# Experts in slots of 256 rows, norm and gate in one phase, weights in two parts, gathers issued three chunks ahead

## The chip, the cores and the metric

The kernel runs on one core of a Trainium2 chip. The core has TensorE (PE), VectorE (DVE), ScalarE (ACT), GpSimd (POOL) and SyncE (SP), which here only issues DMAs, and 16 DMA engines. The metric is the device time of the whole program in microseconds, 4737.4 us before the change (median of three runs, 4737.3 to 4738.18).

## The reference, cut to what matters

The program is four sub-layers over 4096 tokens of 256 values: linear attention, a feed-forward layer, a selective-scan (Mamba) part of two blocks, and a mixture of eight experts. Each is wrapped as `x = x + _layernorm(f(_layernorm(x)))`. Only the closing norm of the third and the fourth are touched:

```python
x = x + _layernorm(_L1_attn_ref(_layernorm(x), ...))
x = x + _layernorm(_L1_ffn_ref(_layernorm(x), ...))

def _L1_ffn_ref(x, W1, b1, W2, b2, Wg, bg):
    gate_scores = softmax(x @ Wg + bg)                 # 8 experts
    h = relu(einsum('btc,ech->bteh', x, W1) + b1)      # 256 -> 1024
    expert_out = einsum('bteh,ehc->btec', h, W2) + b2  # 1024 -> 256
    topk_scores, topk_idx = top_k(gate_scores, 2)
    top_probs = softmax(topk_scores)
    sel = take_along_axis(expert_out, topk_idx[..., None], axis=2)
    return sum(sel * top_probs[..., None], axis=2)
```

Only the two chosen experts of a token need computing.

## The kernel before

Tokens lie in SBUF as `x_res`, 32 tiles of 128 tokens (`NT`), eight chunks of four tiles (`NCH`, `TPC`). Two spare tiles in front hold zeros. The code is written by hand per engine, with semaphores; each phase (`net.run`) ends in a barrier over all engines, in which SP clears the phase's semaphores, and the next begins with SP setting its counting ones to 1. What stands on an engine runs in the written order.

The Mamba part ends with `stream_out` (`normalise_all` with `back`): the parked input is loaded as one DMA, VectorE takes statistics of all 32 tiles (L116, L120), POOL forms the inverse roots (L1383, L1385), VectorE normalises tile by tile into a double buffer (L1403) and POOL adds the residual chunk by chunk (L1391).

`moe_gate` takes one chunk per turn: statistics and norm again on VectorE (L116 to L1511), transposes on TensorE (L1543), copies on ScalarE (L1533), a small fp32 matmul with the gate weights (L1550), logits on VectorE (L1518). Beside it one expert's weights per chunk (2 MB, two DMAs, L1473 and L1475) are split into a bf16 high part by ScalarE (L1530) and a bf16 rest by VectorE (L1515), which makes nearly fp32 products out of three bf16 matmuls. SP also fills the buffer of rows per expert, `slots_x` in HBM, with zeros (36 DMAs, L1483), between the second and the third expert's weights.

`moe_route` forms top-2, shares and, for each token and choice, a row in `slots_x` (`slot`); each expert's rows start at a multiple of 128, so 72 slots of 128 rows (`NSLOT`) always suffice, and `tile_expert` tells the expert of each. `moe_scatter`: VectorE norms a chunk into `c_xn` (L1691), POOL issues two indirect DMAs per tile (L1711), 64 in all.

`moe_experts` runs one slot per turn, 72 turns. On TensorE: two transposes of the next slot's rows (L1785), the first layer as 48 matmuls of 128 columns, weights stationary (L1815: 8 output blocks, 2 halves of the input, 3 products), in two halves of PSUM banks, then the second layer of the slot before as 24 matmuls of 256 columns, `h` stationary (L1797). The expert's number is read into a register, so the weights' addresses are formed by register instructions. ScalarE adds bias and applies relu (L1848), VectorE makes the bf16 high part and rest of `h` (L1881, L1883). POOL stores each result to `slots_y` (L1771).

`moe_combine`: POOL gathers two rows per token by indirect DMA (L1914, 64 issues), one chunk ahead of VectorE, which weighs and adds them (L1942, L1946), takes statistics, waits for POOL's inverse root (L108, L110), normalises (L1955) and adds to `x_res` (L1960). The inverse root of a chunk stands on POOL behind the gathers of the next. At the end one DMA stores all 4 MB (L1996).

## Time and profile before

| what | us |
|---|---|
| median of the runs | 4737.4 |
| the profiled execution's own time | 4734.2 |
| its span | 4732.5 |
| up to the end of the Mamba blocks (untouched) | 3676 |
| closing norm, then gate phase, up to the routing's first DMA | 161.9 |
| routing, up to the first scatter issue | 27.4 |
| scatter, up to TensorE's first instruction of the expert loop | 95.9 |
| expert loop on TensorE | 631.2 |
| from there to the first gather issue | 13.5 |
| gathers and sums, up to the store's issue | 112.5 |
| the store, to the end of the span | 14.0 |
| combine, VectorE per chunk: weighted sums and statistics (4706.11 to 4710.69) | 4.6 |
| combine, VectorE per chunk: norm and addition (4712.34 to 4714.98) | 2.6 |
| combine, POOL: eight gathers and one root, the pitch of a chunk (4628.91 to 4641.54) | 12.6 |
| ScalarE, cast of 128x256 out of PSUM, mean | 0.37 |

The times of stages are differences of start times in the timeline of the one profiled execution. A row's duration is the instruction's own; what an engine waited for stands behind it in brackets. Matmuls overlap, so their pace is read from the difference of their starts, not from their durations.

### The profile page before, as it was taken

How to read it: one execution, taken by the hardware profiler on the slowest of the kernel's cores; microseconds unless marked ns; L12 is line 12 of the kernel's file. 1: busy time of each engine (PE TensorE's matmuls, PEld its weight loads, DVE VectorE, ACT ScalarE, POOL GpSimd, SP SyncE). 2: the span in 40 equal slices, each digit the busy share in tenths (PEclk: the TensorE clock that was granted, in tenths of full speed). 3: DMA queues.
4: the chain of work that ended last, by engine and by line, in shares of the span. 5: the costliest groups of instructions: out<-in, count | busy, mean ns of one | idle time of the engine just before them, and what ended most of it. 6: DMA issues, size and time to landing. Idle time of an engine off the chain costs nothing. (4 is left out here: it accounts for less than half of the span.)

```text
span 4732.5 us, 95080 instructions
## 1 busy us (share of the span) xinstructions
PE 3637.2 (77%) x29740; PEld 2399.9 (51%) x29741; DVE 2779.8 (59%) x4894; ACT 2001.0 (42%) x4694; POOL 2035.8 (43%) x1225
## 2 busy tenths in 40 slices
PE   6888869838988888888569888888888124888870
PEld 3545546525555555555345555555555123666650
DVE  3444423347777777777557777777776542333324
ACT  2121212136666665656256656565664111323220
POOL 1010100026666666667356767676767223000016
PEclk9878769969999999999779999999999557999995
DMA  1000000111213121312121312121221521000003
GB/s 47 0 0 0 0 20 0 35 44 48 73 48 74 48 74 48 74 48 71 33 64 48 74 48 71 49 72 50 65 57 51 204 87 66 29 29 31 29 30 100
DMA packets 156158, 241.76 MB, mean 51 GB/s; under 512 B 26450, under 2 KB 84082, under 8 KB 153076
## 3 DMA queue, kind: packets, MB, share of 16 engines
q1 hardware_dynamic: 146164, 210.61, 16.4%
q0 software_dynamic: 9600, 26.23, 1.6%
q8 instruction: 207, 3.39, 0.3%
q14 instruction: 187, 1.53, 0.1%
HBM read 118.86 MB, written 36.18 MB: 33 GB/s over the span
## 5 line engine op out<-in xcount | busy, mean ns | idle before, releaser
L893 POOL TENSOR_TENSOR m_hc<-m_h,m_Cb 128x1024 f32<-128x1024 f32 x512 | 1204.9, 2354 | 764.5 <-DVE m_h L1014 446.7
L1014 DVE TENSOR_TENSOR_SCAN m_h<-m_dA,m_hlast,m_bank 128x256 f32<-128x256 f32 x2048 | 1355.0, 727 | 142.8 <-PE m_bank L1295 61.5
L1277 PE MATMUL m_bank<-m_hc,ident 128*128 128x512 f32 x2048 | 1206.0, 678 | 146.3 <-POOL m_hc L893 146.0
L1144 ACT ACTIVATE m_dA<-m_delta,m_rate 128x256 f32<-128x256 f32 x2048 | 894.1, 500 | 15.6 <-DVE m_h L1014 14.7
L1293 PEld LDWEIGHTS m_bank<-m_M,m_U 128*128 128x128 bf16 x8192 | 607.6, 101 | 359.9 <-DVE m_h L1014 220.6
L1293 PE MATMUL m_bank<-m_M,m_U 128*128 128x64 bf16 x8192 | 677.9, 197 | 123.5 <-DVE m_h L1014 112.2
L1295 PEld LDWEIGHTS m_bank<-m_M,m_U 112*128 112x128 bf16 x8192 | 581.2, 101 | 204.8 <-issue 172.8
L1295 PE MATMUL m_bank<-m_M,m_U 112*128 112x64 bf16 x8192 | 678.3, 197 | 0.0
L1277 PEld LDWEIGHTS m_bank<-m_hc,ident 128*128 128x128 f32 x2048 | 338.7, 205 | 195.4 <-POOL m_hc L893 162.8
L1771 POOL DMA_DIRECT2D slots_y<-x_y x72 | 39.0, 541 | 609.8 <-DVE x_y L1870 609.8
L962 DVE SCALAR_TENSOR_TENSOR m_cv<-m_xpre,m_conv,m_cv 128x256 f32<-128x256 f32 x384 | 273.5, 754 | 22.5 <-ACT m_cv L1082 18.0
L1207 PE MATMUL m_bank<-m_pair,m_in 128*128 128x256 f32 x1024 | 268.8, 389 | 8.1 <-ACT m_cv L1082 4.4
L1815 PE MATMUL x_bank<-x_xhi,r_wlo 128*128 128x128 bf16 x1152 | 262.3, 228 | 13.4 <-DVE x_xlo L1861 0.4
L1848 ACT ACTIVATE x_h<-x_bank,x_b 128x128 f32<-128x128 f32 x576 | 164.7, 368 | 225.4 <-PE x_bank L1815 225.3
L1207 PEld LDWEIGHTS m_bank<-m_pair,m_in 128*128 128x128 f32 x1024 | 194.7, 194 | 120.2 <-issue 94.1
L1815 PE MATMUL x_bank<-x_xhi,r_whi 128*128 128x128 bf16 x1152 | 250.6, 218 | 0.0
L1815 PE MATMUL x_bank<-x_xlo,r_whi 128*128 128x128 bf16 x1152 | 249.6, 217 | 0.1
L108 POOL TENSOR_SCALAR var_eps<-a_mv 128x4 f32<-128x4 f32 x16 | 3.7, 229 | 520.3 <-DVE a_mv L120 520.3
L1881 DVE CAST x_hhi<-x_h 128x512 bf16<-128x512 f32 x144 | 61.5, 427 | 273.2 <-ACT x_h L1848 273.2
L1797 PE MATMUL x_bank<-r_whi,x_hlo 128*128 x576 | 157.6, 274 | 58.6 <-DVE x_hlo L1883 58.4
L398 PE MATMUL a_bank<-a_qh,a_phi 128*128 128x512 f32 x256 | 142.8, 691 | 48.3 <-DVE a_qh L233 38.8
L844 POOL TENSOR_TENSOR m_Mlo<-m_Mf,m_Mhi 128x1024 bf16<-128x1024 f32 x64 | 166.3, 2598 | 6.6 <-ACT m_Mhi L1125 6.6
(262 smaller groups left out, 5747.6 us busy)
## 6 DMA issues: line engine op xcount, KB each, us to landing
m_Cb<-m_c_rows SPq DMA_DIRECT2D x256, 256.0 KB, 3.2
m_M<-m_Mhi SPq DMA_DIRECT2D x128, 256.0 KB, 4.1
m_M<-m_Mlo SPq DMA_DIRECT2D x64, 256.0 KB, 3.9
m_U<-m_Uhi SPq DMA_DIRECT2D x128, 128.0 KB, 3.2
g_stage<-in_e_w SPq DMA_DIRECT2D x16, 1024.0 KB, 6.9
slots_x<-x_res SPq DMA_DIRECT2D x36, 256.0 KB, 4.2
x_x_in<-slots_x SPq DMA_DIRECT2D x72, 128.0 KB, 2.0
slots_y<-x_y POOLq DMA_DIRECT2D x72, 128.0 KB, 2.0
```

The source lines that it names most:

```text
L844: nc.gpsimd.tensor_tensor(Mlo[:, j], Mf[:, j], Mhi[:, j], ALU.subtract).then_inc(s["mlo_done"], 1)
L893: nc.gpsimd.tensor_tensor(hc[:, n % 2], h[:, n % RING], Cb[:, g % 2, n % NG, :].unsqueeze(1).broadcast_to([P, KI, CM]), ALU.mult).then_inc ...
L962: i = nc.vector.scalar_tensor_tensor(cv[:, m, :], xpre[:, m, k:k + CM], conv[:, m, k:k + 1], cv[:, m, :], ALU.mult, ALU.add)
L1014: nc.vector.tensor_tensor_scan(h[:, n % RING, m, :], dA[:, n % RING, m, :], VB[(n % 2) * 2 + g][:, (m % 2) * CM:(m % 2 + 1) * CM], hlast[: ...
L1144: nc.scalar.activation(dA[:, n % RING, m, :], delta[:, par, m, :], ACT.Exp, scale=rate[:, m, n:n + 1]).then_inc(s["da_done"], 1)
L1207: last = nc.tensor.matmul((H0, H1)[g % 2][:, m % 2 * CM:(m % 2 + 1) * CM], w_in[:, k, m * P:(m + 1) * P], xT[:, k, :], start=(k == 0), sto ...
L1277: last = nc.tensor.matmul(Y[half][:], net.ident[:], hc[:, n % 2, 2 * half:2 * half + 2, :], start=(n == 0), stop=(n == NS - 1))
L1293: nc.tensor.matmul(bank[:, at:at + SUB], U1[:, par, j, m * P:(m + 1) * P], M1[:, par, j, n, :], start=True, stop=False)
L1295: last = nc.tensor.matmul(bank[:, at:at + SUB], U2[:, par, j, m * P:(m + 1) * P], M2[:, par, j, n, :], start=False, stop=True)
L1797: last = nc.tensor.matmul(YB[par][:, 0:D], h_part[:, par, m * P:(m + 1) * P], w_part[:, bass.ts(e * (WB // 2) + KD * KH // 2 + m, D)], sta ...
L1815: last = nc.tensor.matmul(HB[par][b][:, at:at + P], w_part[:, bass.ts(e * WB + kk * KH + m, P)], x_part[:, par, kk * P:(kk + 1) * P], star ...
L1848: last = nc.scalar.activation(h[:, par, m * P:(m + 1) * P], HB[par][b][:, at:at + P], ACT.Relu, bias=b1[:, bass.ts(e * KH + m, 1)])
```

## The change

- **Slots of 256 rows** (`SLOT`), 40 of them; two slots per round, 20 rounds. TensorE runs both first layers (each 48 matmuls of 256 columns in four groups of two output blocks, each group a PSUM bank), each followed by the four transposes of its slot of the next round, then both second layers (each 48 matmuls of 256 columns). Eight banks as before, but `h` is kept in fp32 only for two groups.
- **Norm, residual and gate in one phase**, chunk by chunk, written out without loops: first statistics, root, normalisation on ScalarE in place, residual added by POOL, second statistics, root, rows for the gate. `stream_out` goes. With each chunk goes one 1 MB piece of weights, eight pieces, the first four experts. The zero fills (now 40) are issued behind the last piece.
- **The other eight pieces** are loaded and split in the scatter phase, the subtraction on VectorE (`low`) between the norms of tiles. The scatter goes tile by tile with 12 buffers.
- **Combine**: gathers run three chunks ahead, straight from `slot`, into a buffer for all tiles; VectorE sums chunk c before it finishes chunk c − 1; each finished chunk is stored at once, in place of the one store at the end.

The diff, cut to what matters:

```diff
-    net.run(lambda n: stream_out(n, parked))
...
-NSLOT = 2 * NT + NE
+
+SLOT = 2 * P
+NSLOT = NT + NE
 WB = (KD * HID + KH * D) // P
 IDX = mybir.dt.int32
+EARLY = NE
+
+
+def expert_weights(net, ctx, tag, whi, wlo, pieces):
+
+    dram = net.dram
+    W1 = KD * HID
+    stage = net.sb(ctx, tag + "stage", [P, 2, W1])
+    loaded = [net.own(f"{tag}weights{par}") for par in range(2)]
+    hi_done, lo_done = net.sem(tag + "hi_done"), net.sem(tag + "lo_done")
+    cols = lambda i: slice(pieces[i] * W1, (pieces[i] + 1) * W1)
+
+    def load(sp, i):
+        if i >= 2:
+            sp.wait_ge(lo_done, 1 + i - 1)
+        of = dram[("e_w1", "e_w2")[pieces[i] % 2]][pieces[i] // 2]
+        sp.dma_start(stage[:, i % 2, :], of.rearrange("p a b -> p (a b)")).then_inc(loaded[i % 2], 16)
+
+    def high(act, i):
+        act.wait_ge(loaded[i % 2], (i // 2 + 1) * 16)
+        net.nc.scalar.copy(whi[:, cols(i)], stage[:, i % 2, :]).then_inc(hi_done, 1)
+
+    def low(dve, i):
+        dve.wait_ge(hi_done, 1 + i + 1)
+        net.nc.vector.tensor_tensor(wlo[:, cols(i)], stage[:, i % 2, :], whi[:, cols(i)], ALU.subtract).then_inc(lo_done, 1)
+
+    return load, high, low
...
+                for c in range(NCH):
+                    if c >= 2:
+                        sp.wait_ge(s["sum_done"], 1 + c - 1)
+                    sp.dma_start(residual[:, c % 2], chunk(net.parked, c)).then_inc(s[f"back{c % 2}"], 16)
+                    load(sp, c)
+                sp.wait_ge(s["zero_set"], 1 + 1)
+                filled = slots_x.rearrange("(i p r) d -> i p r d", p=P, r=SPARE)
+                for i in range(NSLOT * SLOT // (P * SPARE)):
+                    sp.dma_start(filled[i], net.x_all[:, 0:SPARE, :]).then_inc(s["zeroed"], 16)
+                sp.wait_ge(s["zeroed"], NSLOT * SLOT // (P * SPARE) * 16)
...
+                def root(c):
+                    pool.wait_ge(s["stats"], 1 + c + 1)
+                    if c == 1:
+                        pool.wait_ge(s["root"], 1 + 1)
+                    elif c >= 2:
+                        pool.wait_ge(s["root2"], 1 + c - 1)
+                    inverse_root(net, pool, rstd[:, c % 2], mv[:, c % 2, :, 1]).then_inc(s["root"], 1)
+
+                def add(c):
+                    pool.wait_ge(s["normal"], 1 + c + 1)
+                    pool.wait_ge(s[f"back{c % 2}"], 16 * (c // 2 + 1))
+                    nc.gpsimd.tensor_tensor(chunk(x, c), chunk(x, c), residual[:, c % 2], ALU.add).then_inc(s["sum_done"], 1)
+
+                def root2(c):
+                    pool.wait_ge(s["stats2"], 1 + c + 1)
+                    pool.wait_ge(s["root"], 1 + min(c + 2, NCH))
+                    pool.wait_ge(s["root2"], 1 + c)
+                    inverse_root(net, pool, chunk2(rstd2, c), chunk(mv2, c)[:, :, 1]).then_inc(s["root2"], 1)
+
+                root(0)
+                root(1)
+                for c in range(NCH):
+                    add(c)
+                    root2(c)
+                    if c + 2 < NCH:
+                        root(c + 2)
...
+                first(0)
+                first(1)
+                shifts(0)
+                for c in range(NCH):
+                    if c + 1 < NCH:
+                        shifts(c + 1)
+                    second(c)
+                    if c + 2 < NCH:
+                        first(c + 2)
+                    low(dve, c)
+                    rows(c)
+                    if c >= 1:
+                        logits(c - 1)
+                logits(NCH - 1)
...
+                normal(0)
+                for c in range(NCH):
+                    if c + 1 < NCH:
+                        normal(c + 1)
+                    high(act, c)
+                    if c >= 1:
+                        turned(c - 1)
+                turned(NCH - 1)
...
-                after(V.tensor_scalar(tiles[:], tiles[:], float(P), -1.0, ALU.mult, ALU.add))
+                after(V.tensor_scalar(tiles[:], tiles[:], float(SLOT), -1.0, ALU.mult, ALU.add))
...
+            def _(pool):
+                for t in range(NT):
+                    pool.wait_ge(ready, 1 + t + 1)
+                    for i in range(2):
+                        nc.gpsimd.indirect_dma_start(slots_x, bass.IndirectOffsetOnAxis(slot[:, t, i:i + 1], 0),
+                                                     xn[:, t % HELD, :], None).then_inc(sent[t % HELD], 16)
...
+                for t in range(NT):
+                    if t >= HELD:
+                        dve.wait_ge(sent[t % HELD], t // HELD * 32)
+                    nc.vector.tensor_scalar(xn[:, t % HELD, :], x[:, t, :], mv[:, t, 0:1], rstd[:, t:t + 1],
+                                            ALU.subtract, ALU.mult).then_inc(ready, 1)
+                    if t >= HELD and t % 2 == 0 and (t - HELD) // 2 < PIECES:
+                        low(dve, (t - HELD) // 2)
+                for i in range((NT - HELD) // 2, PIECES):
+                    low(dve, i)
...
+    PAIRS, T2 = NSLOT // 2, SLOT // P
+    GROUPS = KH // 2
...
+                def layer1(i, par, e, first):
+                    pe.wait_ge(s[f"xlo_done{par}"], 1 + i + 1)
+                    for g in range(GROUPS):
+                        if par == 1:
+                            pe.wait_ge(s["h_done0"], 1 + i * GROUPS + g + 1)
+                        elif not first:
+                            pe.wait_ge(s["h_done1"], 1 + (i - 1) * GROUPS + g + 1)
+                        pe.sem_inc(net.carrier, 1)
+                        for m in (2 * g, 2 * g + 1):
+                            out = HB[g][:, m % 2 * SLOT:(m % 2 + 1) * SLOT]
+                            for kk in range(KD):
+                                for n, (w_part, x_part) in enumerate(PARTS_X):
+                                    last = nc.tensor.matmul(out, w_part[:, bass.ts(e * WB + kk * KH + m, P)],
+                                                            x_part[:, par, kk, :],
+                                                            start=(kk == 0 and n == 0), stop=(kk == KD - 1 and n == 2))
+                        last.then_inc(s[f"h_psum{par}"], 1)
+
...
+                def body(i, first, last_round):
+                    e = [expert(pe, i * 2 + par) for par in range(2)]
+                    for par in range(2):
+                        layer1(i, par, e[par], first)
+                        if not last_round:
+                            turn(i + 1, par, False)
+                    for par in range(2):
+                        layer2(i, par, e[par], first)
+
...
+    LEAD_Q = 3
...
+                for c in range(NCH):
+                    sp.wait_ge(x_done, 1 + c + 1)
+                    tiles = slice(c * TPC, (c + 1) * TPC)
+                    sp.dma_start(out_rows[:, tiles, :], x[:, tiles, :]).then_inc(stored, 16)
+                sp.wait_ge(stored, NCH * 16)
...
+                for c in range(LEAD_Q):
+                    gather(c)
+                for c in range(NCH):
+                    if c + LEAD_Q < NCH:
+                        gather(c + LEAD_Q)
+                    root(c)
...
+                sums(0)
+                for c in range(1, NCH):
+                    sums(c)
+                    result(c - 1)
+                result(NCH - 1)
...
-                sp.dma_start(out.rearrange("(n p) d -> p n d", p=P), net.x).then_inc(stored, 16)
```

How the instructions stand on each engine. On TensorE, at the start of the expert loop, before (`x_xhi`, `x_xlo` are the two parts of the rows, `r_whi`, `r_wlo` those of the weights; ISA and REGISTER_ALU form the address of the weights):

```order
L1785 MATMUL x_bank<-ident,x_x_in 128x128 x2
L1748 TENSOR_LOAD r_tile_expert
L1748 ISA x2
L1785 MATMUL x_bank<-ident,x_x_in 128x128 x2
L1815 ISA
L1815 MATMUL x_bank<-x_xhi,r_wlo 128x128
L1815 REGISTER_ALU
L1815 MATMUL x_bank<-x_xlo,r_whi 128x128
L1815 MATMUL x_bank<-x_xhi,r_whi 128x128
```

and the same place now:

```order
L1879 MATMUL x_bank<-ident,x_x_in 128x128 x8
L1835 TENSOR_LOAD r_tile_expert
L1835 ISA x2
L1835 TENSOR_LOAD r_tile_expert
L1835 ISA x2
L1895 ISA
L1895 MATMUL x_bank<-x_xhi,r_wlo 128x256
L1895 REGISTER_ALU
L1895 MATMUL x_bank<-x_xlo,r_whi 128x256
L1895 MATMUL x_bank<-x_xhi,r_whi 128x256
```

The triple of matmuls is the same with twice the columns; both experts' numbers are read ahead of it.

On VectorE, in the gate phase, one chunk before (`g_st`, `g_mv` are statistics):

```order
L120 BN_AGGR g_mv<-g_st 128x2 x4
L1506 REGISTER_ALU
L1507 ISA
L1507 COPY r_mv<-g_mv 128x8
L1509 ISA
L1509 COPY r_rstd<-g_rstd 128x4
L1511 TENSOR_SCALAR g_xn<-x_res,g_mv,g_rstd 128x256 x4
L1515 ISA
L1515 TENSOR_TENSOR r_wlo<-g_stage,r_whi 128x4096
L1518 ISA
L1518 TENSOR_TENSOR r_gate<-g_bank,g_bg 128x32
```

and one chunk now:

```order
L1555 SCALAR_TENSOR_TENSOR g_shift<-g_mv,g_rstd 128x4
L1562 BN_STATS g_st<-x_res 128x6 x4
L1566 BN_AGGR r_mv<-g_st 128x2 x4
L1546 BN_STATS g_st<-x_res 128x6 x4
L1550 BN_AGGR g_mv<-g_st 128x2 x4
L1442 TENSOR_TENSOR r_wlo<-g_stage,r_whi 128x2048
L1574 TENSOR_SCALAR g_xn<-x_res,r_mv,r_rstd 128x256 x4
L1579 TENSOR_TENSOR r_gate<-g_bank,g_bg 128x32
```

Two statistics blocks stand in a chunk, the first of them (L1562) behind POOL's addition of the residual, and the weights' subtraction is half as long and stands ahead of the rows.

On POOL, in the combine phase, before:

```order
L1914 DMA q_got<-slots_y,q_at 128x256 x8
L1923 UNCONDITIONAL_BRANCH
L1923 ISA
L1914 DMA q_got<-slots_y,q_at 128x256 x8
L1919 REGISTER_ALU
L107 ISA
L108 TENSOR_SCALAR var_eps<-q_mv 128x4
L110 TENSOR_TENSOR q_rstd<-var_eps,minus_half 128x4
```

and now:

```order
L2027 DMA q_got<-slots_y,r_slot 128x256 x32
L107 ISA
L108 TENSOR_SCALAR var_eps<-q_mv 128x4
L110 TENSOR_TENSOR q_rstd<-var_eps,minus_half 128x4
L2027 DMA q_got<-slots_y,r_slot 128x256 x8
```

The first root stands behind 32 gathers instead of 16, and so the root of the fifth chunk behind the last gather.

## Rows read from the trace of the kernel before

**Rows 1.** The page, granted TensorE clock in 40 equal slices, tenths of full speed.
```profile
PEclk9878769969999999999779999999999557999995
```

**Rows 2.** Timeline of VectorE, POOL and SP: start, duration (us), engine, line, operation, releaser.
```profile
3676.16 10.55 DVE L116 BATCH_NORM_STATS2 so_st<-x_res 128x6 f32<-128x256 f32 x32 [5.24 <-PEq L85]
...
3699.95 2.42 DVE L1403 TENSOR_SCALAR so_tmp<-x_res,so_mv,so_rstd 128x256 f32<-128x256 f32 x1
3699.78 2.44 POOL L1391 TENSOR_TENSOR x_res<-so_residual,so_tmp 128x1024 f32<-128x1024 f32 x1 [0.87 <-DVE so_tmp L1403]
...
3727.09 33.68 SPq L1483 DMA_DIRECT2D slots_x<-x_res  x36
3728.35 1.41 DVE L116 BATCH_NORM_STATS2 g_st<-x_res 128x6 f32 x4 [8.76 <-DMA g_bg<-in_e_bg]
3730.77 1.04 POOL L110 TENSOR_TENSOR g_rstd<-var_eps,minus_half 128x4 f32<-128x4 f32 x1
...
3747.58 4.42 DVE L1515 TENSOR_TENSOR r_wlo<-g_stage,r_whi 128x4096 f32 x1
3753.77 0.19 DVE L1518 TENSOR_TENSOR r_gate<-g_bank,g_bg 128x32 f32 x1 [1.76 <-PE g_bank L1550]
...
3838.02 0.34 SPq L1580 DMA_DIRECT2D o_rank<-in_rank  x1
```

**Rows 3.** Busy time of a 5 us window in the fills; last two columns DMA share, GB/s.
```profile
3745.00:3750.00 5.00, 1.96 (x8) 1.57 (x8) 3.79 (x6) 1.07 (x2) 1.04 (x1) 0.50 1.05 403
```

**Rows 4.** Expert loop: its window (PE, PEld, DVE, ACT, POOL, PEclk), two groups, TensorE's timeline.
```profile
3961.30:4592.50 631.20, 541.50 (x5321) 429.15 (x5322) 221.93 (x431) 191.44 (x648) 38.43 (x71) 1.00 0.09 29
...
L1883 DVE TENSOR_TENSOR x_hlo<-x_h,x_hhi 128x512 bf16<-128x512 f32 x144 | 99.7, 693 | 5.0
L1881 DVE CAST x_hhi<-x_h 128x512 bf16<-128x512 f32 x144 | 61.5, 427 | 273.2 <-ACT x_h L1848 273.2
...
4107.67 0.27 PE L1797 MATMUL x_bank<-r_whi,x_hhi 128*128 x1
4108.02 0.41 PE L1785 MATMUL x_bank<-ident,x_x_in 128*128 128x128 f32 x2
4108.53 0.23 PE L1815 MATMUL x_bank<-x_xhi,r_wlo 128*128 128x128 bf16 x1
...
4110.46 0.22 PE L1815 MATMUL x_bank<-x_xhi,r_whi 128*128 128x128 bf16 x1
4110.78 0.23 PE L1815 MATMUL x_bank<-x_xhi,r_wlo 128*128 128x128 bf16 x1
...
4111.02 0.23 PE L1815 MATMUL x_bank<-x_xhi,r_wlo 128*128 128x128 bf16 x1
...
4113.95 0.27 PE L1797 MATMUL x_bank<-r_whi,x_hhi 128*128 x1
...
4114.28 0.27 PE L1797 MATMUL x_bank<-r_whi,x_hhi 128*128 x1
```

**Rows 5.** POOL's timeline in the scatter, its first and its last issue.
```profile
3865.39 1.47 POOL L1711 DMA_INDIRECT slots_x<-c_xn,c_at  x1 [26.70 <-DVE c_xn L1691]
...
3945.79 0.96 POOL L1711 DMA_INDIRECT slots_x<-c_xn,c_at  x1 [0.30 <-issue]
```

**Rows 6.** Combine: timeline of VectorE, POOL and SP.
```profile
4605.96 1.02 POOL L1914 DMA_INDIRECT q_got<-slots_y,q_at  x1 [10.48 <-DVE q_at L1934]
...
4628.85 1.23 DVE L1960 TENSOR_TENSOR x_res<-x_res,q_z 128x1024 f32 x1 [0.16 <-DVE q_z L1955]
4628.91 2.00 POOL L1914 DMA_INDIRECT q_got<-slots_y,q_at  x1 [0.30 <-issue]
...
4700.73 0.95 POOL L1914 DMA_INDIRECT q_got<-slots_y,q_at  x1 [0.30 <-issue]
...
4718.49 0.40 SPq L1996 DMA_DIRECT2D out_x<-x_res  x1
```

537 lines of the change are left out of this document (250 added, 287 removed).

## The prediction

> **What bounds the kernel now.** The profile was read from its coarse views to its fine ones. In the row of the granted clock the reader is to see the last nine of the 40 slices: two at 0.5, one at 0.7, five at 0.9 or more, one at 0.5 [rows 1]. They are the expert part, the only one that the diff touches; attention, feed-forward and Mamba take the 3676 us before. Inside these last 1056 us the timeline gives the stages. The closing norm of the Mamba part starts at 3676.2, the gate phase runs to about 3836, the routing begins at 3838.0 [rows 2], the scatter's DMA issues run from 3865.4 to 3946.8 [rows 5], the expert loop on TensorE from 3961.3 to 4592.5 [rows 4], the gathers from 4606.0 to 4701.7, and one store of 4 MB, issued at 4718.5, fills the rest [rows 6]. Each stage ends in a barrier, so gains add up, and each has its own limit:
>
> - Norm and gate: VectorE, POOL and DMA in turns. A single VectorE TENSOR_SCALAR that normally takes 0.33 us took 2.42 us while POOL added a chunk for 2.44 us [rows 2]: the two exclude each other. 36 fills of 256 KB occupy the queue for 33.7 us, at about 403 GB/s [rows 2, 3], with later weight loads behind them.
> - Scatter and gathers: POOL's issue, 0.96 us busy and 0.30 us idle in the one, 0.95 and 0.30 in the other, so 1.26 and 1.25 us each [rows 5, 6].
> - Experts: TensorE. One turn is 128 rows. A first-layer triple of 128-column matmuls takes 0.25 us (4110.78 to 4111.02), though three bare steps are 0.16 at 128 columns; a second-layer triple of 256 columns takes 0.33 us (4113.95 to 4114.28) [rows 4]. So twice the columns cost only a third more. In the loop the clock is at 1.00, the higher level (2.4 GHz).
>
> **The change, part by part** (all against the profiled run, span 4732.5, own time 4734.2; the median of the runs is 4737.4, 3.2 more, and I take the same difference for the new kernel).
>
> **1. Experts.** Before: 72 turns of 128 rows in 631.2 us, 8.77 each. Now 40 slots of 256 rows, two per round, 20 rounds: 10240 rows instead of 9216, so 11% more padding is paid. Per slot: 16 first-layer triples and 16 second-layer triples, all of 256 columns. The first-layer form with 256 columns is not in the trace. Its bounds are 0.25 us per triple (the 128-column row, which it can't beat) and 0.33 plus the 0.09 by which the 128-column triple exceeds its three bare steps, 0.42. I take 0.327, the second-layer row: the instruction pattern with one register step per triple is the same, and there it costs nothing beside 256 columns. 16 × 0.327 = 5.23 us for either layer. Waits: from the end of one group of matmuls to the next the row shows 0.32 us instead of 0.08 to 0.11 (4110.46 to 4110.78) [rows 4], so +0.22 per wait; three inner ones per slot make 0.66. Transposes: two take 0.51 us until the next matmul (4108.02 to 4108.53), plus 0.24 ahead of them (0.35 from the matmul at 4107.67, less its own 0.11) [rows 4]; four I take as 1.0. One round: 2 × (5.23 + 0.66) + 0.22 + 2 × 1.0 + 2 × (0.22 + 5.23) + 0.6 for branch and register loads = 25.5 us, times 20 = 510 us. **−121 us.** The wait ahead of each second layer for the half of hlo just made goes, since both first layers now stand ahead of both second layers (it needs no term: the round is counted anew). What is late next must be VectorE: cast 0.43 and subtraction 0.69 per group [rows 4], 1.15 us against 1.5 us of TensorE, and 5.2 us of second layer lie ahead of the one that needs the last group. So it stays covered. If it were not, 1 us per round returns, 20 us. Ends: 459 us (no wait costs anything: 4 × 5.23 + 1.7 + 0.35 per round) and 510 + 32 × 20 × 0.09 = 568 us (0.42 per first-layer triple).
>
> **2. Norm, residual and gate in one.** The closing norm with its barrier (3676.2 to 3723.6) disappears as a phase, its work goes into the gate's chunks. First 4.7 us until the small loads land (as 3723.6 to 3728.35), two statistics blocks of 1.83 (1.41 plus the aggregation), root, four normalisations on ScalarE (about 1.5, from 0.37 for a cast of this shape, see the table), one addition 2.44 [rows 2]: the second statistics of chunk 0 start 12.8 us in. Then a cycle through POOL and VectorE: add 2.44, second statistics 1.83, first statistics of the chunk after next 1.83, weights' subtraction 2.25 (half of the 4.42 row), root 1.36, four hops of 0.2: 10.5 us. The subtraction is in it because its two SBUF inputs hold POOL off; the evidence is weaker than for TENSOR_SCALAR, it is the gather that took 2.00 instead of 0.95 us beside a TENSOR_TENSOR [rows 6]. Without it the cycle is 8.3. The SP queue issues the eighth piece after the sixth subtraction, at 12.8 + 5 × 10.5 + 5.9 = 71.2, and only behind it the fills, now 40 instead of 36: 10.5 MB at 403 GB/s are 26.0 us, with the piece before (2.6) and 2.5 until the last lands: 102.3. The last chunk's logits: second statistics at 84.3 (the seventh round is 2 short), 6.8 to the rows' end, 6.4 through transposes and gate matmuls (as 3747.6 to 3753.96): 98. So fills end it, just, and the routing starts at 3676.1 + 102.3 + 2.3 = 3780.7 instead of 3838.0: **−57 us**, ends −47 (cycle 12.5) and −68 (cycle 8.3).
> The Trainium skill, page "SBUF — State Buffer", in the table on the bandwidth-pool intuition, gives HBM to core about 358 GB/s; by it the fills would take 29.3 instead of 26.0 us and the stage would gain 54. The row shows 403, so the sum goes by the row.
>
> **3. Routing.** Two operations shrink from 576 to 320 elements: −0.7 us.
>
> **4. Scatter.** Still 64 issues at 1.27 = 81 us, starting 1 us earlier as one tile is enough to begin. New beside them: 8 MB of weights (20 us of DMA at 403 GB/s, on another queue, landing early), and on VectorE eight subtractions of 2.25 us with two SBUF inputs. The gather at 4628.91 began 0.06 us after such an operation of 1.23 us and took 1.05 us longer [rows 6]; a subtraction that begins while an issue is in flight would hold the next for about 1.7 us. 8 × 1.7 = 14. **+13 us**; ends 0 and +18 (8 × 2.25). What waits behind: the next scatter issues; VectorE has 12 tiles of lead.
> Here a page speaks for another result: the Trainium skill, "SBUF — State Buffer", section "Who interferes with whom", says that a tensor_tensor takes only the read interface of the pair shared with GpSimd while descriptor generation needs the write interface (marked as inferred), so such a DMA would not be stalled. By it this term is −1 and the time 14 less; the 2.00 us row speaks against it.
>
> **5. Combine and store.** POOL issues three chunks ahead. No index copies: first issue at about 4605.2 in old time. 64 × 1.25 = 80, and four roots instead of six ahead of the last gather, each with what it drags along 2.65 us (12.65 us per eight gathers and a root, see the table): ends at 4695.8 instead of 4701.7. But root(4) now stands behind the last gather, and VectorE has more left: root 1.5, results of four chunks at 2.7, sums of two at 4.6 (both from the table), hops: 22.1, ending at 4717.9. Before, the sums ended 3 us earlier, then came a barrier and the store's issue at 4718.5, with 14.0 us to the end of the span. Now only the last 512 KB follow the last sum: 0.2 + 3.5 (1.3 at 403 GB/s, the rest latency, an estimate) + 1.6 for the barrier: 4723.2 against 4732.5. **−9 us**, ends −4 and −14.
>
> **6. Barriers.** About 50 more semaphores are set and cleared on SP, at some 0.05 us each (estimate from stage changes of 1.6 us with about 17 of them and 2.3 with 22); part of it is in the terms: +2 us.
>
> Sum: −121 − 57 − 1 + 13 − 9 + 2 = −173. Span 4559.5, own time about 4561, median 4737.4 − 173 = **4564 us**.
>
> **Rivals.**
> - *TensorE's waits vanish behind longer matmuls.* 256 columns give the sequencer slack of 0.08 us per triple, and it may run ahead past a met wait. Against it: before each turn, after 24 such matmuls, there is still a gap of 0.24 (with a register load in it). Experts 459: 4564 − 51 = 4513.
> - *The register step stays visible with 256 columns,* as weights rather than moving operand depend on it. Against: the step is short of the slack. 568: 4564 + 58 = 4622.
> - *A TENSOR_TENSOR does not hold POOL off:* scatter 14 less, gate cycle 8.3 instead of 10.5, which brings the fills 11 forward: 4539. The 2.00 us row [rows 6] speaks against it, gathers beside two-input SCALAR_TENSOR_TENSOR that lose nothing speak for it. The Trainium skill's rule for the scatter is the one named in part 4.
> - *Slower than before: TensorE falls to the lower of its two clocks (1.2 GHz, granted 0.5) in the expert loop.* Matmuls are 418 us of the 510; at half clock 836, total 928: 4982. The point is a mean granted clock of 0.71, where 418/0.71 + 92 reaches the 683 us that eat the whole gain. In the old loop it is at 1.00 [rows 4] although TensorE idles 1 us in each turn; the new one idles less. Hence small.
> - *The change does not do what it says:* a weight piece or a gather that is not covered holds its stage. The largest would be the eight late pieces outside the scatter, 8 × (2.6 + 1.8 + 2.25) = 53 us: 4617. They need 35 us of an 81 us stage.
>
> **How the numbers follow.** Forecast 0.66 (4535 to 4600), waits vanish 0.12, the register step 0.07, POOL not held off 0.09, uncovered pieces 0.03, clock 0.02, other 0.01. The range takes the first four cases nearly whole: 4510 to 4620. Something near 0.2% is what a measurement can tell here. Faster 0.97, same 0.01, slower 0.02.
>
> **What would show it.** Right: second-layer and first-layer triples both near 0.33, a round near 25.5 us, 20 rounds near 510; fills that start about 71 us into the gate stage and end it; scatter issues of up to 3 us beside subtractions; a VectorE tail of about 22 us after the last gather; a last store of 512 KB. Wrong: a triple at 0.25 or above 0.4, gate cycles of 8, scatter issues all at 0.96, a granted clock below 1 in the loop.

## The result, and the profile after

The changed kernel takes **4497.4 us** (median of 4 runs, 4491.8 to 4501.8) against 4737.8 us (4 runs, 4737.3 to 4746.5) for the kernel before on the same chip: ratio 0.9487, 95% interval 0.9473 to 0.9501, 240 us less. Forecast were 4564 us and a range of 4510 to 4620. The direction was right, the size was not: 67 us more were gained, 13 us beyond the range's end. The profiled execution took 4501.8 us, with a span of 4500.1 us and a mean granted clock of 0.866.

The granted clock of the changed kernel, in 40 slices of 112.5 us, to be held against [rows 1]; the last seven and a third of the one before are its expert part:

```profile
PEclk8888878968999999999978999999999985599995
```

The time in front of the expert part varies from one execution to the next, although no kernel here touches it: in the profiles of this case Mamba's last addition ends between 3667.1 and 3689.3 us. So stages are compared from that point on. Each figure is read from the traces of before and after; the first row counts from the end of that addition, the last one to the end of the span, all else from start to start.

| Stretch | before | after | difference | forecast |
|---|---|---|---|---|
| end of Mamba's last addition to the routing's first DMA | 167.1 | 108.1 | −59.0 | −57 and part of +2 |
| to the first scatter issue | 27.4 | 25.1 | −2.3 | −2 |
| to TensorE's first work of the expert loop | 95.9 | 108.8 | +12.9 | +14 |
| expert loop on TensorE, to its last matmul | 631.9 | 449.7 | −182.2 | −121 |
| to the first gather | 12.8 | 11.4 | −1.4 | 0 |
| first gather to the end of the span | 126.5 | 117.2 | −9.3 | −9 |
| sum | 1061.6 | 820.3 | −241.3 | −173 |

Five of six lines hit to within 3 us. **The expert loop alone missed, by 61 us.** The window view of both loops (length, then busy us and instructions of PE, PEld, DVE, ACT and POOL, granted clock, DMA share, GB/s), before and then after; the last line is one whole round of after, from the start of one round's first matmul to that of the next:

```profile
3961.30:4593.40 632.10, 542.40 (x5328) 429.78 (x5328) 221.93 (x431) 191.44 (x648) 38.43 (x71) 1.00 0.09 29
```

```profile
3921.80:4371.70 449.90, 443.90 (x4000) 393.36 (x4000) 227.88 (x399) 153.30 (x360) 21.13 (x39) 0.99 0.14 45
4105.80:4128.09 22.29, 22.00 (x200) 19.55 (x201) 11.40 (x21) 7.66 (x18) 1.08 (x2) 1.00 0.14 47
```

Before, TensorE was busy for 542 of 632 us, after for 444 of 450, and for 22.00 of 22.29 in a round. The clock is the higher level (2.4 GHz) in both, but for the first stretch of each loop: in after the first 28 matmuls of the first layer start 0.213 us apart at a granted 0.50, later ones 0.109 at 1.00. The timeline of after's TensorE shows where the idle time is gone (start, duration, line, operation; the rows to look at are the starts of a first layer, its transposes and what follows them; where rows are left out, triples repeat every 0.33 us):

```profile
4105.80 0.28 PE L1895 MATMUL x_bank<-x_xhi,r_wlo 128*128 128x256 bf16 x1 [0.30 <-issue]
4106.14 0.27 PE L1895 MATMUL x_bank<-x_xhi,r_wlo 128*128 128x256 bf16 x1
...
4110.72 0.27 PE L1895 MATMUL x_bank<-x_xhi,r_wlo 128*128 128x256 bf16 x1
4110.94 0.27 PE L1895 MATMUL x_bank<-x_xhi,r_whi 128*128 128x256 bf16 x1
4111.05 0.60 PE L1879 MATMUL x_bank<-ident,x_x_in 128*128 128x128 f32 x4
4111.48 0.27 PE L1895 MATMUL x_bank<-x_xhi,r_wlo 128*128 128x256 bf16 x1
...
4116.72 0.60 PE L1879 MATMUL x_bank<-ident,x_x_in 128*128 128x128 f32 x4
4117.16 0.27 PE L1908 MATMUL x_bank<-r_whi,x_hlo 128*128 x1
```

The 16 triples of a first layer take 5.25 us (4105.80 to 4111.05) and no wait between them shows; the four transposes take 0.43 us until the next matmul; the only gap of a round stands at its start, where two experts' numbers are loaded: 0.30 us of idle engine, and 0.43 us more from one matmul's start to the next than elsewhere. Round: 5.25 + 5.24 + 10.48 for the matmuls, 2 × 0.44 + 0.43, together 22.3 us, the pitch at which rounds start in the trace.

The gate stage of after, one cycle of VectorE and POOL (in square brackets the idle time ahead of an instruction and what ended it), to be held against [rows 2]:

```profile
3716.61 1.39 DVE L1562 BATCH_NORM_STATS2 g_st<-x_res 128x6 f32<-128x256 f32 x4
...
3720.61 2.29 DVE L1442 TENSOR_TENSOR r_wlo<-g_stage,r_whi 128x2048 bf16<-128x2048 f32 x1 [0.50 <-ACT r_whi L1438]
3720.72 3.20 POOL L110 TENSOR_TENSOR g_rstd<-var_eps,minus_half 128x4 f32<-128x4 f32 x1
...
3722.82 3.45 DVE L1574 TENSOR_SCALAR g_xn<-x_res,r_mv,r_rstd 128x256 f32<-128x256 f32 x4
3722.93 0.33 SPq L1434 DMA_DIRECT2D g_stage<-in_e_w  x1
3723.78 2.34 POOL L1520 TENSOR_TENSOR x_res<-x_res,g_residual 128x1024 f32<-128x1024 f32 x1
...
3726.36 1.39 DVE L1562 BATCH_NORM_STATS2 g_st<-x_res 128x6 f32<-128x256 f32 x4
```

One cycle is 9.75 us (3716.61 to 3726.36). POOL's TENSOR_TENSOR of the root, 1.04 us when alone, takes 3.20 beside the subtraction; four TENSOR_SCALARs, 1.38 us when alone, take 3.45 beside POOL's addition.

### The profile page after: what moved, and what is told of

Same layout as the page of the kernel before. It is cut to its first block and busy times, and to the rows that moved or that the text cites. A ratio compares the mean times of both kernels' runs of the same rounds, so it can differ in the third digit from the quotient of the medians.

```text
span 4500.1 us, 88368 instructions
## 1 busy us (share of the span) xinstructions
PE 3545.9 (79%) x28412; PEld 2364.2 (53%) x28413; DVE 2771.5 (62%) x4814; ACT 1979.1 (44%) x4446; POOL 2045.3 (45%) x1206
## 5 line engine op out<-in xcount | busy, mean ns | idle before, releaser
L1949 ACT ACTIVATE x_h<-x_bank,x_b 128x256 f32<-128x256 f32 x320 | 134.1, 470 | 285.8 <-PE x_bank L1895 278.2
L1863 POOL DMA_DIRECT2D slots_y<-x_y x40 | 21.7, 542 | 446.2 <-DVE x_y L1990 446.2
L1895 PE MATMUL x_bank<-x_xhi,r_wlo 128*128 128x256 bf16 x640 | 176.1, 275 | 6.0 <-issue 5.0
L1895 PE MATMUL x_bank<-x_xlo,r_whi 128*128 128x256 bf16 x640 | 175.8, 275 | 0.0
L1895 PE MATMUL x_bank<-x_xhi,r_whi 128*128 128x256 bf16 x640 | 175.8, 275 | 0.0
L1908 PE MATMUL x_bank<-r_whi,x_hhi 128*128 x640 | 174.4, 273 | 0.0
L1908 PE MATMUL x_bank<-r_wlo,x_hhi 128*128 x640 | 174.4, 273 | 0.0
L1908 PE MATMUL x_bank<-r_whi,x_hlo 128*128 x640 | 174.4, 273 | 0.0
```

Source lines behind the costliest of these rows:

```text
L1895: last = nc.tensor.matmul(out, w_part[:, bass.ts(e * WB + kk * KH + m, P)], x_part[:, par, kk, :], start=(kk == 0 and n == 0), stop=(kk == ...
L1908: last = nc.tensor.matmul(YB[par][:, t * D:(t + 1) * D], h_part[:, par, m, t * P:(t + 1) * P], w_part[:, bass.ts(e * (WB // 2) + KD * KH / ...
L1949: last = nc.scalar.activation(h[:, g % 2, m % 2, :], HB[g][:, m % 2 * SLOT:(m % 2 + 1) * SLOT], ACT.Relu, bias=b1[:, bass.ts(e[par] * KH + ...
```

## The experiments

Twelve kernels were run. First the expert loop, since it holds the miss.

**Theory** formed from the trace of after: TensorE has two limits, its stream of instructions and the columns that its matmuls pass. In the old first layer the stream was the slower one (0.25 us for each triple with its register steps), so that every wait and register load came on top. With 256 columns the matmuls are the slower one (0.327), the stream runs ahead, and what it has beside matmuls vanishes. **Rivals:** the gain comes from the order of the round (two first layers ahead of two second ones), or waits became cheap for another reason.

**Half the columns, shared addresses.**

```diff
+ for half in range(2):
+     rows = slice(half * P, (half + 1) * P)
      for kk in range(KD):
          for n, (w_part, x_part) in enumerate(PARTS_X):
-             last = nc.tensor.matmul(out, w_part[:, bass.ts(e * WB + kk * KH + m, P)], x_part[:, par, kk, :], ...)
+             last = nc.tensor.matmul(out[:, rows], w_part[:, bass.ts(e * WB + kk * KH + m, P)], x_part[:, par, kk, rows], ...)
```

> The new kernel with every first-layer matmul of 256 columns split into two of 128 (96 instead of 48 per slot, same products, same weights loaded twice). Theory A (the old first layer was paced by its instructions, 0.25 us per triple whatever the columns below 256): 32 triples of 0.25 per slot instead of 16 of 0.327, 8.0 instead of 5.2 us, plus waits between groups that show again at 0.2 us each; over 40 slots the expert loop grows from 450 to about 560 to 590 us. Theory B (the gain of the loop comes from the new order of the layers, not from the wider matmuls): the columns are the same, the loop stays within 10 us of 450.

Measured: 4510.9 us, ratio 0.9517 (0.9475 to 0.9559); expert loop 456.7 instead of 449.7 us. A triple of 128 columns now starts every 0.17 us (TensorE's timeline):

```profile
4109.01 0.22 PE L1897 MATMUL x_bank<-x_xhi,r_wlo 128*128 128x128 bf16 x1
...
4109.18 0.22 PE L1897 MATMUL x_bank<-x_xhi,r_wlo 128*128 128x128 bf16 x1
...
4109.34 0.22 PE L1897 MATMUL x_bank<-x_xhi,r_wlo 128*128 128x128 bf16 x1
```

This looked as if my theory had fallen: the same 128 columns, and no 0.25. But the order of TensorE's instructions shows what the edit did beside it. The second half reuses the addresses of the first, so a pair of register steps (one ahead of the first matmul of a triple, one behind it) stands only in the first two of the four triples of an output block. A round's first rows fit: there the triples with the pair start 0.25 and 0.22 us apart, the first matmul of each 0.11 ahead of the second, where 0.06 is usual, and the even 0.17 comes behind them:

```profile
4108.37 0.23 PE L1897 MATMUL x_bank<-x_xhi,r_wlo 128*128 128x128 bf16 x1 [0.29 <-issue]
4108.48 0.22 PE L1897 MATMUL x_bank<-x_xlo,r_whi 128*128 128x128 bf16 x1
...
4108.62 0.23 PE L1897 MATMUL x_bank<-x_xhi,r_wlo 128*128 128x128 bf16 x1
...
4108.84 0.22 PE L1897 MATMUL x_bank<-x_xhi,r_wlo 128*128 128x128 bf16 x1
```

The run changed two things at once and told nothing on the pair. So a second run gave each half a register of its own.

**Half the columns, an address pair for each triple.**

```diff
  def layer1(i, par, e, first):
+     e1 = (e, expert(pe, i * 2 + par))
      ...
-     w_part[:, bass.ts(e * WB + kk * KH + m, P)]
+     w_part[:, bass.ts(e1[half] * WB + kk * KH + m, P)]
```

> The changed kernel with its first layer in halves of 128 columns, as in the earlier run with halves, but the second half computes its weight addresses from a register of its own: one pair of register steps for each triple of matmuls, as in the kernel before; the earlier run shared a pair between two triples. One more register load per slot comes with it. Theory A (TensorE's own instruction stream paces the old first layer; a register pair takes about 0.17 us of it, three matmuls alone little): every triple of 128 columns at 0.25 us, a slot's first layer at 8.0 instead of 5.3, the expert loop 40 x 2.7 = 110 us above the changed kernel's 450 us, so 550 to 570. Theory B (something else in the old loop, its PSUM banks or its waits, made the triple 0.25): triples stay at 0.165, the loop within 20 us of 457.

Measured: 4671.9 us, ratio 0.9854 (0.9827 to 0.9881); expert loop **618.9 us**, 162 more than with shared addresses and nearly the 631.9 of the old kernel. Timeline of its TensorE, one first layer:

```profile
4109.69 0.23 PE L1898 MATMUL x_bank<-x_xhi,r_wlo 128*128 128x128 bf16 x1
...
4109.94 0.23 PE L1898 MATMUL x_bank<-x_xhi,r_wlo 128*128 128x128 bf16 x1
...
4110.18 0.23 PE L1898 MATMUL x_bank<-x_xhi,r_wlo 128*128 128x128 bf16 x1
...
4110.70 0.23 PE L1898 MATMUL x_bank<-x_xhi,r_wlo 128*128 128x128 bf16 x1
...
4117.39 0.63 PE L1879 MATMUL x_bank<-ident,x_x_in 128*128 128x128 f32 x4
...
4118.44 0.23 PE L1898 MATMUL x_bank<-x_xhi,r_wlo 128*128 128x128 bf16 x1 [0.42 <-issue]
```

Triples are back at 0.25 us. And with them everything else is back: from one group to the next 0.52 instead of 0.25 us, so 0.27 for the wait; from the transposes to the next matmul 1.05 instead of 0.43 us. Per slot 32 × 0.087 = 2.8, three waits 0.8, transposes with the register loads 0.6, together 4.2 against 162.2 / 40 = 4.05 us measured. Theory A's 550 to 570 us was thus too low. The waits' surplus was expected in neither theory's number (110 us), but it follows from the first: a stream that paces the loop exposes all it holds. The sizes I had put into the forecast, 0.22 for a wait and 1.0 for the transposes, are those of such a loop.

The two runs bound the stream's costs, by this reading. Four triples with four pairs take 1.0 us, with two pairs no more than 0.66, so a pair costs at least 0.17 us and three matmuls at most 0.08 of the stream.

**More waits, in the changed kernel and in the one before.** TensorE waits again, for something long done, and increments a semaphore behind it, as at a group's start: four more times per slot in the one (160 in all), six more per turn in the other (432). A wait below is always the two together.

```diff
  # after, ahead of each m
+ if m % 2:
+     pe.wait_ge(s[f"xlo_done{par}"], 1 + i + 1)
+     pe.sem_inc(net.carrier, 1)
  # before, ahead of each m
+ if m % (KH // 2):
+     pe.wait_ge(s["xlo_done"], 1 + k + 1)
+     pe.sem_inc(net.carrier, 1)
```

> The new kernel with one more wait that is already met, and one more semaphore increment, in the middle of each first-layer group on TensorE: 4 more per slot, 160 in all. If a met wait costs 0.22 us wherever it stands (the prediction's step), the loop grows by 35 us to 485. If the sequencer runs ahead behind matmuls of 256 columns, it stays within 3 us of 450.

> The old kernel with the same addition ahead of each output block of the first layer but the first of a half: 6 per turn, 432 in all, behind matmuls of 128 columns. If the price of a met wait shows only where TensorE is paced by its instructions, the loop grows by about 0.2 x 432 = 90 us, from 631 to 720. If a met wait costs nothing in either kernel and the 0.22 us gap has another cause (the change of bank), it stays at 631.

Measured: after 4511.3 us, loop 457.9 (+8.2, **0.05 us** per wait); before 4807.7 us, ratio 1.0143 (1.0083 to 1.0203), loop 700.2 (+68.3, **0.16 us** per wait). The first lies between the two forecasts of 453 and 485, the second near the 720 of its first one. A step from one output block (m) to the next in the old kernel, and the places at which the new one lets a gap show (0.18 to 0.19 where a step is 0.11, at most once in four triples, at a group's start):

```profile
4100.37 0.23 PE L1818 MATMUL x_bank<-x_xhi,r_wlo 128*128 128x128 bf16 x1
...
4100.77 0.23 PE L1818 MATMUL x_bank<-x_xhi,r_wlo 128*128 128x128 bf16 x1
```

```profile
4107.86 0.27 PE L1898 MATMUL x_bank<-x_xhi,r_whi 128*128 128x256 bf16 x1
4108.05 0.28 PE L1898 MATMUL x_bank<-x_xhi,r_wlo 128*128 128x256 bf16 x1
```

In the old kernel each wait shows. In the new one, by the same reading of the two limits, four triples have 4 × (0.327 − 0.25) = 0.31 us of slack: one wait fits, two of 0.16 to 0.22 just don't, and 0.07 us of them shows. A met wait is thus not free behind 256 columns; it has a budget, and the changed kernel stays within it.

**The order of the round.** Each slot's second layer stands right behind its first layer and the next transposes, instead of both first layers ahead of both second ones.

```diff
  for par in range(2):
      layer1(i, par, e[par], first)
      if not last_round:
          turn(i + 1, par, False)
- for par in range(2):
      layer2(i, par, e[par], first)
```

> The new kernel with the second layer of a slot directly behind its first layer and the transposes. The last group's relu (0.84), cast and subtraction (1.2) and two hops then stand between first and second layer, less the transposes' 0.45: about 2 us per slot, 80 us over 40 slots. Theory A (pace of instructions is the main source of the gain): the loop grows to about 530 us, and the old kernel's own wait for the subtraction, 58 us, is the part of the gain that order explains. Theory B (order is the main source): the loop loses most of its 181 us gain, 600 us or more.

Measured: 4625.3 us, ratio 0.9758 (0.9717 to 0.98); loop 566.9, +117.2 us or 2.93 per slot. The waits of its TensorE (total us, times, longest), of a stretch with 37 slots:

```profile
PE x_bank L1908 <- DVE x_hlo L1980: 88.7, 37, 2.8
PE x_bank L1895 <- issue: 4.9, 17, 0.3
```

The loop lies between the two theories' 530 and 600 us. 105 of the 117 us stand between the transposes and the second layer, 2.63 per slot, most of it the way of the last group through ScalarE and VectorE (the view counts 2.40 as idle, as it lets the transposes' ends run on). Another 13 us lie inside the second layers: behind some of the pauses the granted clock was 0.50, the lower level, and about 130 matmuls start 0.21 instead of 0.11 us apart (4302.3 to 4305.4, 4316.1 to 4319.2 and others). So the order is needed: without it a good part of the gain is gone. The rival is thus true in part. The kernel before had its second layer a turn late and still waited for the halves of h, as the same view of its loop shows (here of a stretch with 66 such waits):

```profile
PE x_bank L1797 <- DVE x_hlo L1883: 54.7, 66, 0.9
```

That is 0.83 us per turn, and it is gone in the changed kernel, which has no wait for x_hlo in its loop.

**The loop's account.** With an address pair for each triple, and all else of the changed kernel, 128 rows take 618.9 / 80 = 7.74 us against 8.78 before: order, groups and the lost wait give 72 × 1.04 = 75 us. The 8 more half slots (40 × 2 against 72 turns) take back 8 × 7.74 = 62. Sharing the address gives 162, and 256 columns in one matmul instead of twice 128 give 7. Together −182 us, as measured. By this account the step from 128 to 256 columns is worth 169 us, and nearly all of it is the half as many register pairs and what they had exposed. The trace agrees: between the run with shared addresses and the one with an address for each triple, 135 of the 162 us lie inside the first layers, and most of the rest where they begin, behind the transposes and at the start of a round.

**VectorE's subtraction beside POOL.** Two edits leave the subtraction out of one stage; the low halves of those eight weight pieces are zero then, set by ScalarE. First beside the scatter:

```diff
- if t >= HELD and t % 2 == 0 and (t - HELD) // 2 < PIECES:
-     low(dve, (t - HELD) // 2)
  ...
  for i in range(PIECES):
      high(act, i)
+     blank(act, i)
```

> The new kernel without the eight subtractions of VectorE in the scatter phase: ScalarE writes zeros to the low parts of the last four experts' weights instead, so that the result is less exact. If the subtractions hold POOL's issues off (eight issues of 2.1 to 2.8 instead of 0.96 us), the 64 issues take 81 us again and the time falls by 12 to 13 us. If they cost through DMA traffic of the weights, which is unchanged here, it stays.

Measured: 4493.3 us, ratio 0.9474 (0.9444 to 0.9504); from the first scatter issue to the last 80.0 instead of 92.1 us, 12.1 less or 1.51 per subtraction. The issues of the scatter in after, beside the subtraction at 3821.47, and then the row of all scatter issues without it (shortest, median and longest in ns):

```profile
3820.88 0.96 POOL L1778 DMA_INDIRECT slots_x<-c_xn,r_slot  x1 [0.30 <-issue]
3822.14 2.44 POOL L1778 DMA_INDIRECT slots_x<-c_xn,r_slot  x1 [0.30 <-issue]
3824.89 2.54 POOL L1778 DMA_INDIRECT slots_x<-c_xn,r_slot  x1 [0.31 <-issue]
3827.73 0.96 POOL L1778 DMA_INDIRECT slots_x<-c_xn,r_slot  x1 [0.30 <-issue]
```

```profile
L1781 POOL DMA_INDIRECT slots_x<-c_xn,r_slot x64: 956/961/1248, 3819.9 to 3899.9; - x64
```

The page "SBUF — State Buffer" of the Trainium skill, section "Who interferes with whom", has such a DMA unstalled beside a tensor_tensor (it marks the reason as inferred). Here it is stalled; the measurement decides.

The same in the gate stage, twice: first with ScalarE zeroing the halves in the gate stage itself, then with the zeroing moved to the scatter stage.

```diff
  # the first attempt
- low(dve, c)         # VectorE
+ blank(act, c)       # ScalarE, behind high(act, c)
  # the second
- low(dve, c)
+ skip(dve, c)        # the wait and the semaphore of low, without the subtraction
```

> The same in the gate phase for the first eight pieces (low parts written as zeros by ScalarE). If POOL's root and addition wait for the subtraction, the cycle of a chunk falls from 9.75 to about 8 us, the fills start 9 to 11 us earlier and the time falls by about 10. If the cycle is set by something else it stays near 9.75.

> The changed kernel with the weights' subtraction left out of the gate stage on VectorE (only its wait and its semaphore stay); the low halves of these eight pieces are set to zero by ScalarE in the scatter stage, where it has room, so that no engine of the gate stage gets work in exchange. The result lacks these low parts. Theory A (the subtraction takes 2.3 us of VectorE and holds POOL's root for 2.2 us, so that the addition falls on the normalised rows): the gate cycle falls from 9.75 us to about 7.5, the fills start 12 to 16 us earlier and the stage ends with the last logits, about 15 us earlier. Theory B (the cycle runs through ScalarE and TensorE anyway): the cycle falls by less than 1 us, the stage by less than 7.

The first attempt measured 4496.6 us, ratio 0.9496 (0.9474 to 0.9519), and a cycle of 10.6 us, longer than with the subtraction. It was a poor experiment: ScalarE's zeroing (1.91 us a piece) lies in a chain from ScalarE's copy of the turned rows through TensorE and VectorE's logits back to ScalarE. Its timeline, and then that of the second attempt, one cycle each:

```profile
3702.79 1.40 DVE L1565 BATCH_NORM_STATS2 g_st<-x_res 128x6 f32<-128x256 f32 x4
...
3706.68 1.91 ACT L1445 ACTIVATE r_wlo<-g_stage 128x2048 bf16<-128x2048 f32 x1
...
3713.21 0.19 DVE L1582 TENSOR_TENSOR r_gate<-g_bank,g_bg 128x32 f32<-128x32 f32 x1 [5.55 <-PE g_bank L1640]
3713.39 1.40 DVE L1565 BATCH_NORM_STATS2 g_st<-x_res 128x6 f32<-128x256 f32 x4
```

```profile
3725.21 1.40 DVE L1566 BATCH_NORM_STATS2 g_st<-x_res 128x6 f32<-128x256 f32 x4
3733.83 0.19 DVE L1583 TENSOR_TENSOR r_gate<-g_bank,g_bg 128x32 f32<-128x32 f32 x1 [0.99 <-PE g_bank L1641]
3734.01 1.40 DVE L1566 BATCH_NORM_STATS2 g_st<-x_res 128x6 f32<-128x256 f32 x4
```

The second attempt: 4497.1 us, ratio 0.9486 (0.9461 to 0.9511); the cycle is 8.80 us instead of 9.75, the fills start 8.1 us earlier and the scatter 7.8 us earlier. So a subtraction is worth 1 us in the gate stage, not its 2.3, because the chain through TensorE is only 1 us shorter than VectorE's: the logits' instruction (3725.03) and a shift of 0.15, then on ScalarE 2.08 (norm), 1.88 (high part of the weights) and 1.06 (turned rows), then 3.58 of gate matmuls, for which the next logits wait. The cycle falls by less than 1 us, as theory B had it; the stage by a little more than its 7.

**What can still be gained.** Fills between the weight loads, and each chunk's root ahead of the next gathers, first alone, then both; last with four instead of eight weight pieces in the gate stage.

```diff
  # gate stage, sync queue
+ if c >= 1:
+     for i in range((c - 1) * FILLS // (NCH - 1), c * FILLS // (NCH - 1)):
+         sp.dma_start(filled[i], net.x_all[:, 0:SPARE, :]).then_inc(s["zeroed"], 16)
  # combine, gpsimd
+ root(c)
  if c + LEAD_Q < NCH:
      gather(c + LEAD_Q)
- root(c)
  # the last of the four runs
- EARLY = NE
+ EARLY = NE // 2
- if t >= HELD and t % 2 == 0 and (t - HELD) // 2 < PIECES:
-     low(dve, (t - HELD) // 2)
+ if HELD <= t < HELD + PIECES:
+     low(dve, t - HELD)
```

> The new kernel with the 40 zero fills issued behind the weight pieces 1 to 7, five or six each, instead of behind the last. DMA is busy for a third of a cycle there. If the fills bound the gate phase, it ends with the last logits, about 8 us earlier. If the fills delay the residual and the weights by 3.5 us per chunk and the chain has no slack for it, the cycle grows and the gain is lost.

> The new kernel with the inverse root of chunk c ahead of the gathers of chunk c + 3 instead of behind them. The tail of VectorE behind the last gather is 21 us now; with one root more ahead of the last gather (2.7 us) it should shrink to about 14: 4 to 5 us less in all. If the tail is set by the gathers' landing, nothing changes.

> The changed kernel with both edits that gained alone: the fills issued between the gate stage's weight loads, and the root of each chunk ahead of the next gathers. From the end of the Mamba part to the end of the span they gave 811.4 and 815.5 us against 820.3. If they add up, 806.5 here, and 14 us less than the changed kernel in the median; if the earlier routing makes the one edit worth nothing, 811.

> Fills between the weight loads and roots first, as in the run below, and only four weight pieces instead of eight in the gate stage; the other twelve beside the scatter, one subtraction behind each of the tiles 12 to 23. If a subtraction costs 1.5 us of POOL's time beside the scatter, four more cost 6 us there; four gate cycles without one gain 4 x 2 = 8 us if the cycle falls to 7.7. So 0 to 5 us faster than the run below; slower by 5 to 10 if the twelve pieces do not arrive in time behind the tiles.

| Kernel | median us | ratio, 95% | Mamba's end to the scatter | scatter issues | last gather to the end | Mamba's end to the end |
|---|---|---|---|---|---|---|
| changed kernel | 4497.4 | 0.9487 (0.9473–0.9501) | 133.2 | 92.1 | 26.8 | 820.3 |
| fills between | 4487.1 | 0.9474 (0.9452–0.9496) | 125.1 | 92.2 | 26.8 | 811.3 |
| root first | 4489.8 | 0.9488 (0.946–0.9515) | 133.2 | 91.6 | 19.4 | 815.4 |
| both | 4488.0 | 0.9458 (0.9435–0.9481) | 125.1 | 92.6 | 19.4 | 807.2 |
| both, four early | 4488.1 | 0.9463 (0.9441–0.9485) | 119.1 | 98.4 | 19.4 | 806.9 |

The rows come from three chips; each ratio is against the kernel before on the same chip, so the medians are not to be compared by the microsecond. Inside the traces the two edits give 9.0 and 4.8 us and together 13.1, so they add up; in the traces the four forecasts (8, 4 to 5, together 806.5 left, and 0 to 5) all hold to within 1 us. The root first shortens the tail by 7.3 us and lengthens the gathers from 90.4 to 93.2. Four pieces moved gain 6.1 us ahead of the scatter and lose 5.8 in it (4 × 1.51 = 6.0): nothing. The issues of the fills in the changed kernel, and with them between the loads (first and last start):

```profile
L1502 SPq DMA_DIRECT2D slots_x<-x_res x40: 355/646/1548, 3752.6 to 3781.6; - x40
```

```profile
L1505 SPq DMA_DIRECT2D slots_x<-x_res x40: 344/542/967, 3681.3 to 3748.5; - x40
```

The last logits of that run are done at 3769.86 us, 21 us after the last fill's issue, and now end the stage. In the medians these gains of 5 to 13 us are near the spread of single runs (4476 to 4498 for both together), which comes mostly from the part ahead of Mamba's end. The version with both edits is the one to keep, by its trace; by its runs alone its interval overlaps that of the changed kernel.

## Why the prediction was right and wrong

- **What bounds the kernel: mostly right.** Of TensorE it said that twice the columns cost a third more, which held. It read the 0.25 us of a triple off [rows 4] without asking which of two limits that was, and this is the root of the miss.
- **Experts, −121 forecast, −182 measured: wrong.** The step that failed is the working of the round, "+0.22 per wait" and all that was counted like it. Its triples were right: 0.327 us in both layers. Nine waits (1.98 us, of which nothing shows), the transposes (2 × 1.0 where 0.44 was measured, 1.1 too many) and the branch with its register loads (0.6 against 0.43) were sizes of a loop paced by instructions, carried into one paced by columns. They make 3.2 us per round, 25.5 against 22.3, and 64 us in 20 rounds. 3.7 us came back, from ends that I had not counted: 2.9 us pass before the first round's first layer, and that round takes 24.9 us, since its first 28 matmuls run at the lower clock level; the last two rounds, the very last without transposes, are 1.9 us short together.
- **The argument against the right rival failed too.** "Before each turn, after 24 such matmuls, there is still a gap of 0.24" was taken as proof that a wait shows behind 256 columns. But there [rows 4] a register load stood with it, and the stream can have had little lead, since the turn's first layer was paced by it (this is a reading; no run takes that gap apart). In the changed kernel a gap with register loads is left too, 0.43 us, once per round. The rival named the mechanism, got 0.12, and at 459 us was itself 9 too high, since it took the transposes at 0.85.
- **The register step beside 256 columns:** right, it does not show.
- **VectorE stays covered behind the first layers:** right, no wait for x_hlo stands in the waits of the loop, and the run with the other order shows what it would have cost.
- **Norm and gate, −57 forecast, −59 measured: right,** though two misses cancel in it. The cycle was 9.75 instead of 10.5 us, and so the fills start 66.7 us after the stage's first DMA instead of 71.2; from there to the routing it is 35.3 us instead of 33.4. The reason given was half right. The subtraction does hold POOL's root, by 2.2 us, but it is worth only 1 us per cycle, since a chain through ScalarE and TensorE of 8.8 us, not in my working, lies right below. The fills end the stage, as forecast: the last starts at 3781.6, the last logits at 3777.4. Their rate was 388 to 406 GB/s in windows of 5 us from 3758 on, in line with [rows 3] and above the 358 of the Trainium skill, page "SBUF — State Buffer", table on the bandwidth-pool intuition.
- **Scatter, +14 forecast for the stretch from its first issue, +12.9 measured: right** (the +13 of the sum contains 1 us by which it starts earlier), with 12.1 us for eight subtractions, 1.51 instead of 1.7 each. The row of one gather of 2.00 us [rows 6] was enough to turn down the rule of the Trainium skill, page "SBUF — State Buffer", section "Who interferes with whom"; the run without the subtraction confirms it.
- **Combine and store, −9 forecast, −9.3 measured: right,** with a VectorE tail of 21.3 us behind the last gather:

```profile
4473.32 0.95 POOL L2027 DMA_INDIRECT q_got<-slots_y,r_slot  x1 [0.30 <-issue]
...
4475.71 1.38 DVE L2073 TENSOR_SCALAR q_z<-q_z,q_mv,q_rstd 128x256 f32<-128x256 f32 x4 [5.01 <-POOL q_rstd L110]
...
4494.35 1.23 DVE L2078 TENSOR_TENSOR x_res<-x_res,q_z 128x1024 f32<-128x1024 f32 x1
```

- **Barriers, +2:** the stage's first DMA is issued 6.1 us after Mamba's last addition instead of 5.2, the first work on VectorE waits for small loads as forecast; too small to tell apart.
- **The range** took the rivals' times, but not the case that a rival's mechanism holds and its own size is off as well. Its low end stood 3 us below the rival; measured were 16 below it.

## What to carry to other kernels

Ask of every matmul sequence which of two limits paces it, columns or the instruction stream, before its waits are priced: where the stream paces, each wait (here 0.16 to 0.27 us) and each register pair (at least 0.17) adds to the time; where columns do, they are free up to the slack (here 0.08 us per three matmuls of 256 columns). Loops with addresses from registers should pass more columns per address, or share one address among several matmuls; the latter gives 457 us where the same matmuls with an address each take 619. And an experiment that is to change one thing must be looked at in the order of instructions first: one edit here halved the register steps as well, and another moved its work onto the engine that ended the cycle.

## What the runs showed of the hardware

- Register steps are dear on TensorE: 162 us in this loop lie between one pair per three matmuls and one pair per six, of 128 columns, with the waits and register loads that come to show beside them.
- A VectorE TENSOR_TENSOR with two SBUF inputs of 2048 elements (2.28 us) makes a POOL indirect DMA issue take 2.1 to 2.8 us instead of 0.96, which costs the row of issues 1.51 us each time, and a POOL TENSOR_TENSOR 3.20 instead of 1.04. Four VectorE TENSOR_SCALARs beside a POOL addition take 3.45 instead of 1.38 us.
- At the lower of TensorE's two clocks (granted 0.50) matmuls of 256 columns start 0.213 instead of 0.109 us apart. The clock stood there at the start of the changed kernel's loop, after 119 us of idle, and in places in the run with the other order, where TensorE paused 2.4 us ahead of each second layer.
- What precedes the change, the same program in all of them, ended at 3667 to 3689 us in 14 profiles. A gain of 10 us in 4500 is seen in stages inside a trace, not in four runs.
